# Score and maximum matmuls of an attention kernel written as four of 32 output rows each

## What is computed

```
x = x + 0.5 * ffn(layernorm(x))
x = x + attn(layernorm(x))
x = x + 0.5 * ffn(layernorm(x))

attn:  q, k, v = sign(W) x * scale          # 32, 8, 8 heads of width 16; each k, v head serves 4 q heads
       p   = softmax(q k^T / sqrt(16))      # over 1024 keys
       out = sign(W_o) (p v) * scale
```

## Time and profile before

| | us |
|---|---|
| median of 3 runs | 1193.02 |
| lowest and highest of them | 1190.93, 1193.94 |
| the profiled execution | 1191.72 |
| its span, first to last instruction | 1189.9 |

### The profile page before, as it was taken

One profiled execution on the slowest core, in us unless ns is written; L12 is line 12 of the kernel. 1 busy time (PEld: TensorE's weight loads), 2 busy tenths in 40 slices (PEclk: granted clock), 3 DMA queues, 4 the chain that ended last, 5 costly groups with the idle time before them and its releaser, 6 DMA issues.

```text
span 1189.9 us, 16268 instructions
## 1 busy us (share of the span) xinstructions
PE 1078.8 (91%) x5968; PEld 482.1 (41%) x5968; DVE 840.7 (71%) x1146; ACT 732.4 (62%) x1361; POOL 282.8 (24%) x461
## 2 busy tenths in 40 slices
PE   3868687799999999999999999999999999998847
PEld 2656564233423342334333433333333334333335
DVE  3564648777787778787778778878887787773174
ACT  3363733375776677676667676766775676668511
POOL 5034436610241023130032004200500130032010
PEclk9999989699999999999999999999999999999979
DMA  7012132211021102200301131113001200200300
GB/s 247 18 54 85 53 107 91 67 41 43 26 59 30 39 25 63 62 25 26 79 26 26 26 87 30 32 30 77 27 26 49 54 27 26 78 6 6 89 0 36
DMA packets 87360, 59.42 MB, mean 50 GB/s; under 512 B 44145, under 2 KB 73329, under 8 KB 87281
## 3 DMA queue, kind: packets, MB, share of 16 engines
q1 hardware_dynamic: 87280, 58.39, 17.4%
HBM read 37.64 MB, written 20.32 MB: 49 GB/s over the span
## 4 chain that ended last, share of the span: by engine, by line
PE 76%; DVE 10%; ACT 7%; POOL 4%; issue 3%; POOLq 0%; DVEq 0%
PE ps_out L1279 20%; PE ps_score L1267 17%; PE ps_max L1242 16%; PE ps_fill L1200 6%; DVE neg_max L1053 3%; ACT probs L815 2%; PE ps_fill L1227 2%; PE ps_out L1200 2%; PE ps_fill L1185 2%; PE ps_fill L1173 1%; PE ps_fill L1204 1%; PE ps_fill L1217 1%; PE ps_max L1256 1%; ACT xt_h L755 1%; DVE att L1082 1%
## 5 line engine op out<-in xcount | busy, mean ns | idle before, releaser
L815 ACT ACTIVATE probs<-ps_score 128x512 f32<-128x512 f32 x992 | 538.4, 596 | 258.4 <-PE ps_score L1267 257.2
L1053 DVE TENSOR_REDUCE neg_max<-ps_max 128x1 f32<-128x1024 f32 x480 | 572.1, 1220 | 169.9 <-PE ps_max L1242 167.8
L1267 PE MATMUL ps_score<-qst,kst 99*128 99x512 bf16 x992 | 307.4, 385 | 6.3 <-ACT probs L815 4.2
L1242 PE MATMUL ps_max<-kst,qst 96*128 96x512 bf16 x1024 | 290.2, 384 | 15.0 <-DVE neg_max L1111 9.6
L1279 PE MATMUL ps_out<-probs,v_ring 128*32 128x512 f32 x2048 | 273.6, 606 | 3.5 <-ACT probs L815 3.3
L1267 PEld LDWEIGHTS ps_score<-qst,kst 99*128 99x128 bf16 x992 | 77.7, 97 | 263.1 <-ACT probs L815 221.3
L1242 PEld LDWEIGHTS ps_max<-kst,qst 96*128 96x128 bf16 x1024 | 88.6, 98 | 141.5 <-DVE neg_max L1111 19.2
L674 POOL CAST shift<-neg_max 128x16 bf16<-128x16 f32 x32 | 7.1, 221 | 476.3 <-DVE neg_max L1053 476.3
L1279 PEld LDWEIGHTS ps_out<-probs,v_ring 128*32 128x32 f32 x2048 | 40.3, 108 | 96.3 <-issue 87.3
L750 ACT ACTIVATE xn<-xc,ln_shift,rstd 128x512 f32<-128x512 f32 x48 | 38.4, 811 | 47.0 <-POOL ln_shift L585 46.9
L1200 PE MATMUL ps_fill<-wb_h,xt_h 128*128 128x512 f32 x96 | 51.3, 534 | 1.3 <-DVE xc L1040 0.8
(11 more groups left out here) (219 smaller groups left out, 1310.3 us busy)
## 6 DMA issues: line engine op xcount, KB each, us to landing
qst<-q_dram SPq DMA_DIRECT2D x192, 64.0 KB, 2.2
q_dram<-zm SPq DMA_DIRECT2D x24, 256.0 KB, 2.6
kst<-k_dram SPq DMA_DIRECT2D x192, 32.0 KB, 2.2
xc<-x SPq DMA_DIRECT2D x8, 512.0 KB, 4.1
x_dram<-xc SPq DMA_DIRECT2D x8, 512.0 KB, 2.9
xc<-x_dram SPq DMA_DIRECT2D x8, 512.0 KB, 4.4
out<-xc SPq DMA_DIRECT2D x8, 512.0 KB, 3.1
att_dram<-att SPq DMA_DIRECT2D x31, 128.0 KB, 2.2
```

Source lines behind the costliest of these rows:

```text
L815: act.activation(probs[:, kt % 2, j, :], score_bank(i, uu, j), ACT.Exp, scale=1.0 / HD ** 0.5).then_inc(probs_ready, 1)
L1053: dve.tensor_reduce(neg_max[:, uu % 2, t:t + 1], ps_max[max_slot(uu, pos)][:, :, :], AXY, ALU.max, negate=True).then_inc(max_read, 1)
L1242: last = pe.matmul(ps_max[slot][:, half, :], qst[0:SR, r, j, q * P:(q + 1) * P], kst[0:SR, r, half * 512:half * 512 + 512], start=True, st ...
L1267: pe.matmul(score_bank(i, uu, j), kst[0:SR + PARTS, uu, kt * P:(kt + 1) * P], qst[0:SR + PARTS, uu, j, :], start=True, stop=True).then_inc ...
```

## The change

Each score and each maximum matmul becomes four matmuls of 32 output rows into the four quarters of the same bank, with the same moving operand; the semaphore is counted by the last of them. On ACT, the copy of the last unit's output moves from between exps 1 and 2 of a unit's first slot to behind exp 3.

```diff
@@ ACT, body
                     exp_tile(i, uu, kt, 0)
                     exp_tile(i, uu, kt, 1)
-                    if kt == 0 and not (first and uu == 0):
-                        copy_out(i, uu - 1)
                     for item in plan.get(2 * slot - 1, []):
                         fill(item)
                     exp_tile(i, uu, kt, 2)
                     exp_tile(i, uu, kt, 3)
+                    if kt == 0 and not (first and uu == 0):
+                        copy_out(i, uu - 1)
                     for item in plan.get(2 * slot, []):
                         fill(item)
@@ TensorE, max_matmul
-                last = pe.matmul(ps_max[slot][:, half, :], qst[0:SR, r, j, q * P:(q + 1) * P],
-                                 kst[0:SR, r, half * 512:half * 512 + 512], start=True, stop=True)
+                for c in range(0, P, 32):
+                    last = pe.matmul(ps_max[slot][c:c + 32, half, :], qst[0:SR, r, j, q * P + c:q * P + c + 32],
+                                     kst[0:SR, r, half * 512:half * 512 + 512], start=True, stop=True)
                 if half == 1:
                     last.then_inc(max_scores, 1)
@@ TensorE, score
-                pe.matmul(score_bank(i, uu, j), kst[0:SR + PARTS, uu, kt * P:(kt + 1) * P],
-                          qst[0:SR + PARTS, uu, j, :], start=True, stop=True).then_inc(scores_ready, 1)
+                bank_j = score_bank(i, uu, j)
+                for c in range(0, P, 32):
+                    last = pe.matmul(bank_j[c:c + 32, :], kst[0:SR + PARTS, uu, kt * P + c:kt * P + c + 32],
+                                     qst[0:SR + PARTS, uu, j, :], start=True, stop=True)
+                last.then_inc(scores_ready, 1)
```

## The result

The changed kernel takes 1203.0 us (median of five runs, 1200.9 to 1205.0), the kernel before 1193.0 (five runs, 1190.2 to 1193.9): ratio 1.008, 95% interval 1.0055 to 1.0105. The profiled execution took 1203.9 us with a span of 1202.1, which is 12.2 more than the span before.

A forecast was written before the change was run, and what follows sets the result against it. TensorE was taken to bound the kernel, its own work 2.83 of 2.885 us in a slot without filler. Terms +47.6 - 49.4 + 41.5 + 1 - 3 - 4 - 1 + 1 = +33.7 gave 1225 us, range 1180 to 1250.

The forecast's parts named there:

- term 1: Score and maximum groups in the 256 slots: each group of four costs 0.024 us more than one matmul, +47.6 us.
- last two units: Units without maximum matmuls: loop through exp 0.08 us shorter, -1 us; the same term gives the start +1 us.
- What four side by side cost: P times V's passes, 0.455 us against 0.43: 0.025 a group read as operand reading, so 0.240 per bf16 group.
- Term 2: Around P times V: two changes of shape fall away per slot, 256 x 0.19, -49.4 us.
- Term 3: 166 filler pieces, still 128 wide: two changes and partly unhidden weight loads, 0.25 us each, +41.5 us (31 to 58).
- Rival A: Score and maximum matmuls: a bf16 group of four costs one matmul's 0.216 us; 1172 to 1182 us, faster; chance 0.15.
- Term 5: 56 slots without fillers: the wait for exp goes, loop 2.73 us against TensorE's work 2.83, -3 us.
- Term 6: Output copy behind the exps: 14 slots gain 0.06 us, six with a filler copy 0.55, together -4 us.
- Term 4: The turn in each unit's second slot has a change behind it too, but TensorE also waits for VectorE: +1 us.
- Rivals C: Score and maximum groups: four bf16 streams can't be read at 2.4 GHz, 0.455 us a group; about 1660 us; chance 0.10 with D.
- D: Dispatch of 80 records a slot is the bound, 0.09 us each; up to 2290 us; chance 0.10 with C.
- no shape saved: Slots keep their 0.19 us since 96 or 99 rows count as another shape; 1239 or 1281 us; chance 0.07.

The follow-up runs named there:

- e4: Kernel before with only the maximum matmuls written four by 32, scores 128 wide, copy in its old place: 1265.2 us, ratio 1.0594.
- e5b: Changed kernel with the first maximum group put between scores 3 and 4 of a slot: 1194.1 us, ratio 1.0014.
- e1: Kernel before with only the copy of the output moved behind exps 2 and 3: 1193.5 us, ratio 1.0003.

## Why the forecast was right in sign and wrong in size

The sign was luck. Without term 1, the price of a group, which the runs don't show, the recorded sum is 33.7 - 47.6 = -14 us, a faster kernel; it is slower because of costs that no term had, first of all a wait of 9 us. And by the forecast's own sign of being wrong, plain slots of 2.7 us or less, it was wrong: they take 2.67.

Term by term, each with what it measured in the loop (the slots by class, above; 0.275 taken for a piece, and 140 slots with a piece):

```
term                                        forecast   measured
1  price of a group of four, 1984 x           +47.6        0     (0.2155 a group)
2  two changes of shape fewer, 256 x          -49.4      -59     (0.230 a slot, not 0.19)
3  filler pieces, 166 x (171 counted)         +41.5      +47     (0.25 transposes, 0.30 f32r)
4  the turn, beyond terms 1 to 3               +1         +4     (30 slots)
5  slots without fillers, the wait for exp     -3         +1     (0.067 before, 0.085 after)
6  the copy, beyond terms 1 and 2              -4         +1.5   (20 slots)
7  last two units                              -1         +1
-  new wait for exp 2, slots with a piece       0        +10     (0.07 x 140)
-  gain of terms 1 and 2 that did not land      0         +4.6   (25 slots without fillers)
-  rest of the slots with a piece               0         -2
   loop                                      +32.7        +8.1
7  ahead of the loop                           +1      +2 to +4
```

- **The step that failed is "What four side by side cost"**, and with it term 1. I saw four f32 matmuls 0.455 apart where one wide f32 matmul has 0.43, and gave the 0.025 to the group. It belonged to the change of shape: it goes when the neighbours are narrow (0.432 between the passes of 703.90 and 704.34) and comes back in e4 (0.453). What the runs showed in its place is a bf16 group at 0.2155 in a row, the time of one wide matmul, where I had 0.240: 0 in place of +47.6. So P times V had no price to hand on to the bf16 groups. That 0.025 lay close to the 27 ns estimated for a weight load was chance: the four loads are there in every kernel, the 0.025 is not. The row at the lower clock, 0.86 with nothing on top, fits neither reading, since that P times V stands behind wide scores as well; the runs leave it open. The pace that "only the 2.4 GHz array waits for" is not shown.
- **Term 2 was too small for the same reason**: 0.23 a slot, two changes at 0.115. Terms 1 and 2 together were forecast as -2 and measured -59. (The recorded 49.4 is 256 x 0.193; with 0.19 as written it is 48.6.)
- **Term 3 had the right mechanism and nearly the right size.** The bounds 0.19 and 0.35 hold both kinds of piece, and the transposes give the 0.25 that the text said to look for at "a maximum group to a filler and back". That filler slots would grow by 0.2 to 0.3 was wrong (0.09), since their removed changes were worth more than the groups cost.
- **The new wait was in no term and no rival.** I wrote down one loop through ScalarE (score 3, exps 3 and 4, score 2) and not the other (score 1, exps 1 and 2, score 4). It had 0.18 of slack: from score 1 to score 4 TensorE took 0.22 + 0.32 + 1.00 + 0.22 = 1.75, the way through the exps 0.43 + 0.49 + 0.65 = 1.57. TensorE's way is now 0.22 + 0.22 + 0.86 + 0.22 = 1.51. By e5b the wait costs 9 us, nearly all that the kernel lost; 7.6 of it lie in the 118 slots with one or two pieces and no turn, 0.064 each.
- **Rival A had the group's price but not the sum**: it gave 1172 to 1182. On top of its terms came the wait for exp 2, the 0.275 of a piece near the middle of its bounds, and gain that did not land. Of the 71 slots without fillers, 46 gained 0.21 each; the other 25 gained 0.7 us together, 4.6 short. The trace says where they stand. In nine of them (2.844 in place of 2.885) ScalarE's copy of a filler's transposes is queued ahead of exp 3, which starts 1.46 into the slot where it is 1.31 in others (the slot at 369.22):

```profile
370.20 0.61 ACT L755 ACTIVATE xt_h<-ps_fill 128x512 fp32r<-128x512 f32 x1
370.68 1.82 ACT L815 ACTIVATE probs<-ps_score 128x512 f32<-128x512 f32 x3
```

- Twelve more are six pairs, in which the third maximum group waits for a reduction of VectorE; its three reductions run there from 630.86 to 634.32 without a gap (the slot at 630.99):

```profile
633.25 0.62 PE L1243 MATMUL ps_max<-kst,qst 96*32 96x512 bf16 x8 [0.28 <-DVE neg_max L1053]
```

- The last four stand beside a long conversion on ScalarE (L806, L809), two of them with a wait for a reduction of 0.52. By these rows ScalarE's copy takes 1.5 of the 4.6 us, VectorE's pace 2.1 and the four 1.0. That is read from the trace; no run changed that work. In the window the waits of the maximum groups' weight loads for reductions grew from 12.6 to 24.2 us in all, partly beside running matmuls, so the growth is no time of the kernel.
- **Term 5** had its loop right: forecast 2.73 with a group at 0.240, 2.71 in rival A, 2.66 in e5b. In the changed kernel the other loop came first, at 2.67. **Term 6**: the copy slots fell by 3.1 us in all where I had 4. The 14 went from 3.083 to 3.021, as forecast (3.02), the six from 3.573 to 3.199, 0.37 where I had 0.55. But most of this is the narrow groups' doing: with the copy in its old place (e2) the same slots take 2.963 and 3.455, so the move costs 14 x 0.058 and gives 6 x 0.256, a gain of 0.7 us. (The +1.5 of the table is what these slots lack of term 2's gain.) **Term 4** and the last units cost 3 and 2 us more than I had; I did not follow them further.
- **Ahead of the loop**: the five kernels with narrow maxima there start the loop at 236.4 to 242.4 us, the four with wide ones at 233.4 to 236.1, and the medians less the loop differ by some 2 us. The scatter is as wide as the effect.
- **Rivals C, D and "no shape saved" are out**: a group takes 0.2155, 80 records in a slot of 2.67 us are one per 33 ns without a gap, and each removed change is saved. Where VectorE has nothing but its two reductions it bounds no slot, as the text had it.

By the Trainium skill (TensorEngine Tiling (Array Packing), Key Properties) a change of the tiling mode drains TensorE; the runs agree in that each change costs time, 0.115 here, part of which is a weight load that is no longer hidden. By the Trainium skill (TensorE: Matmul & The Clock Gate, Part 3, Measured speedup vs the span model) each further tile adds some 4 ns to the span of one matmul. The starts in a row of groups are 3 to 4 ns apart, which agrees; but a group behind another group costs 0.2155 and nothing on top, so in a row that cost is hidden.

## What to carry to other kernels

Splitting a bf16 matmul with 512 columns into four column tiles was free on TensorE where its neighbours were split too; what costs is each border between split and whole work (0.115 us, and more where the first weights behind it are f32). So count borders per stretch of the schedule, and choose the shape by the neighbours: here narrow where no filler stands and wide around the fillers gave 1.3%, narrow everywhere lost 0.8%. And an effect seen in one place (a longer pass) need not belong to the instruction that shows it: look at the same instruction among other neighbours. When TensorE gets faster between two of its own waits, write down every loop through another engine with its slack, not only the one that binds now.

## What the runs showed of the hardware that was not expected

- Four bf16 matmuls side by side, 96 or 99 rows by 32 columns by 512, take 0.2155 us in a row at the upper level of the clock (granted 1.00 from 320 to 1078), the same as one 128 wide. Their records start 3 to 4 ns apart; the four of P times V behind wide work start some 7 ns apart, 20 ns over the four, in all 256 slots of the kernel before.
- The weights of the next group of four load while this group streams, also from bf16 to f32 (703.69 for a P times V at 703.90), but never across a change between 32 and 128 wide: there the load starts when the first matmul's record does (700.03 in the earlier trace rows; at most 5 ns ahead of it in all 509 changes of the loop before and all 389 of the changed one), and that record can be longer (0.50 instead of 0.39 at 563.96).
- The second matmul behind a change is late too if its weights are f32 or f32r: by 0.05 for transposes and by 0.11 for f32r.
- Slots repeat to a few ns between executions and between kernels: in e1 the slots with maxima and without the copy or the turn are, class by class, within 1 ns of the kernel before in the mean. So single slots could be compared across kernels where whole executions differ by several us, much of it ahead of the loop, which started between 233.4 and 242.4 us.
